# Attention values and probabilities held as rounded part and remainder side by side, multiplied head by head

## The reference

```python
def _L0_xattn_ref(x, context, ln_gamma, ln_beta, w_q, w_kv, w_out, b_out, gate):
    xn = _layernorm(x, ln_gamma, ln_beta)
    q = (xn @ w_q).reshape(B, SQ, NUM_HEADS, DIM_HEAD)
    k, v = jnp.split(context @ w_kv, 2, axis=-1)
    ...
    scores = jnp.einsum('bqhd,bkhd->bhqk', q * SCALE, k)
    attn = jax.nn.softmax(scores, axis=-1)
    out = jnp.einsum('bhqk,bkhd->bqhd', attn, v).reshape(B, SQ, INNER)
    return (out @ w_out + b_out) * jnp.tanh(gate[0])

x = x + jnp.tanh(g_xattn[0]) * _L0_xattn_ref(_layernorm(x, axis=-1), ctx_1024, ...)
```

## Time and profile before

| | us |
|---|---|
| median of three runs | 1162.66 |
| lowest and highest of them | 1161.47, 1164.37 |
| the profiled execution: device time | 1161.57 |
| the profiled execution: span of its trace | 1159.8 |
| busy in the span: PE / PEld | 1075.9 / 930.8 |
| busy in the span: DVE / ACT / POOL | 773.1 / 631.4 / 519.8 |

### The profile page before, as it was taken

The page is one execution under the profiler, slowest core; times in us unless marked ns, Lnnn a source line. Parts: engine busy times, 40 slices in busy tenths (PEclk is TensorE's granted clock), DMA queues, the critical chain, the costliest instruction groups (busy, mean ns, idle before and its releaser), DMA issues.

```text
span 1159.8 us, 22342 instructions
## 1 busy us (share of the span) xinstructions
PE 1075.9 (93%) x7361; PEld 930.8 (80%) x7361; DVE 773.1 (67%) x1963; ACT 631.4 (54%) x1676; POOL 519.8 (45%) x745
## 2 busy tenths in 40 slices
PE   3889999999999999999999999999999779899995
PEld 3688888888888888888788888888887668789983
DVE  2544677767676767776676777676766665686665
ACT  2533556555656565655556565656564545555650
POOL 3512345453535454454535354536354404565441
PEclk9989999999999999999999999999999888999998
DMA  5395882010101011010001010101000522234469
GB/s 150 96 329 207 309 297 63 5 34 9 30 27 31 27 31 35 23 35 22 23 16 32 8 38 9 31 9 31 5 18 9 176 83 78 99 108 152 133 198 287
DMA packets 82382, 95.82 MB, mean 83 GB/s; under 512 B 9291, under 2 KB 74445, under 8 KB 82272
## 3 DMA queue, kind: packets, MB, share of 16 engines
q1 hardware_dynamic: 41904, 44.94, 13.5%
q10 hardware_dynamic: 31520, 32.51, 7.9%
q0 software_dynamic: 8848, 16.96, 4.2%
HBM read 41.98 MB, written 52.39 MB: 81 GB/s over the span
## 4 chain that ended last, share of the span: by engine, by line
PE 61%; DVE 16%; ACT 10%; issue 6%; DMA 4%; POOL 3%; SPq 1%; DVEq 0%; ACTq 0%; POOLq 0%
PE ps_kv L1568 14%; PE ps_ot L1854 8%; PE ps_ot L1668 5%; PE ps_kv L1650 5%; PE ps_s L1811 5%; PE ps_pt L1821 5%; ACT prob L938 4%; DVE negmax L1467 3%; PE ps_pt L1780 3%; PE ps_ot L1793 3%; DVE pT_lo L1478 2%; DVE k_lo L1152 2%; ACT v_hi L928 2%; DMA zb<-places 2%; PE ps_ot L1712 2%
## 5 line engine op out<-in xcount | busy, mean ns | idle before, releaser
L855 POOL TENSOR_TENSOR prob<-prob,rinv 112x750 f32<-112x750 f32 x128 | 185.4, 1448 | 310.7 <-DVE rinv L1472 310.4
L938 ACT ACTIVATE prob<-ps_s,negmax 112x375 f32<-112x375 f32 x256 | 144.7, 570 | 236.4 <-DVE negmax L1467 236.4
L1478 DVE TENSOR_TENSOR pT_lo<-ps_pt,pT_hi 125x672 fp32r<-125x672 f32 x128 | 109.7, 857 | 77.0 <-ACT pT_hi L1051 77.0
L1568 PE MATMUL ps_kv<-ctxT_hi,wkv 128*128 128x376 f32 x512 | 141.6, 357 | 7.8 <-DVE v_lo L1156 3.8
L1467 DVE TENSOR_REDUCE negmax<-ps_s 112x2 f32<-112x750 f32 x128 | 119.0, 930 | 0.1
L1156 DVE TENSOR_TENSOR v_lo<-ps_kv,v_hi 125x512 fp32r<-125x512 f32 x96 | 66.4, 692 | 77.2 <-ACT v_hi L928 77.2
L1568 PE MATMUL ps_kv<-wkv,ctxT_hi 128*125 128x512 f32 x384 | 112.2, 414 | 3.6 <-DVE n_e L1116 2.3
L1821 PE MATMUL ps_pt<-ident,prob 112*125 112x112 f32 x768 | 104.9, 273 | 1.3 <-POOL prob L855 1.3
L814 POOL DMA_INDIRECT places<-ysb,place_i x72 | 70.3, 976 | 69.1 <-ACT ysb L1010 55.9
L1051 ACT ACTIVATE pT_hi<-ps_pt 125x672 fp32r<-125x672 f32 x128 | 93.5, 730 | 9.0 <-PE ps_pt L1821 1.0
L1821 PEld LDWEIGHTS ps_pt<-ident,prob 112*125 112x125 f32 x768 | 95.1, 191 | 1.7 <-POOL prob L855 1.7
(11 more groups left out here) (298 smaller groups left out, 2623.8 us busy)
## 6 DMA issues: line engine op xcount, KB each, us to landing
rows_by_expert<-stage_w ACTq DMA_DIRECT2D x16, 1920.0 KB, 7.3
xg<-rows_by_expert SPq DMA_DIRECT2D x72, 128.0 KB, 2.1
zb<-places SPq DMA_DIRECT2D x16, 448.0 KB, 15.0
arena<-in_L_ffn_mlp_w SPq DMA_DIRECT2D x24, 256.0 KB, 4.4
ctx_in<-in_ctx SPq DMA_DIRECT2D x16, 375.0 KB
acc<-in_L_xattn_w_kv SPq DMA_DIRECT2D x4, 512.0 KB, 13.1
stage_w<-in_L_ffn_mlp_w SPq DMA_DIRECT2D x8, 256.0 KB, 3.0
x_in<-in_x SPq DMA_DIRECT2D x16, 112.0 KB, 2.1
```

The source lines that it names most:

```text
L855: e_prob.done(eng.tensor_tensor(prob[0:TQ, p % 2, :, :], prob[0:TQ, p % 2, :, :], rinv[:, 2 * p:2 * p + 2].unsqueeze(2).broadcast_to([TQ, ...
L938: e_exp.done(eng.activation(prob[0:TQ, p % 2, half, :], S[0:TQ, half, 0:SK], ACT.Exp, bias=negmax[:, h:h + 1], accum_out=rowsum[:, h:h + 1]))
L1478: e_pt_lo.done(eng.tensor_tensor(pT_lo[:, :, :, :].rearrange("p h k t -> p h (k t)"), PT[0:KEYT, :, 0:NKEY * TQ], pT_hi[:, :, :, :].bitcas ...
L1568: last = eng.matmul(out_, lhs(i, k), rhs(j, k), start=(n == 1), stop=(n == KT * len(PASSES)))
```

## The change

The three passes are folded into the shape of the operands. `v_hi` and `v_lo` become one tile `vx`, in which the 64 columns of a head's rounded part stand beside the 64 of its remainder; `pT_hi` and `pT_lo` become one tile `pT`, with 112 columns of the rounded part beside 112 of the remainder, for each head and key tile. One matmul for a head and a key tile then gives a 128 x 224 result of four blocks: hi·hi, hi·lo, lo·hi, and lo·lo, which isn't used. A pair takes 2 x 3 = 6 matmuls of the same size, where there were 9.

The three blocks that count have to be added, and stand in different partitions and columns of PSUM. ACT copies the block lo·hi of both heads (partitions 64 to 127, 64 x 224 in all) into `o_part`, which lies in unused partitions of the tile `b2_all`, in place of its two copies of 64 x 112. DVE gets three new instructions for a pair: `o_part` = hi·lo + `o_part` (64 x 224), then, after a wait on its own semaphore `s_co`, `oT` = hi·hi + `o_part` for each head (64 x 112 each). They stand behind `pT_lo` of the following pair, in slot 2p + 5. `e_oT` is now signalled by DVE.

```diff
-        v_hi = t("v_hi", [128, NKEY, INNER], F32R)
-        v_lo = t("v_lo", [128, NKEY, INNER], F32R)
+        vx = t("vx", [128, NKEY, NH, 2, DH], F32R)
-        pT_hi = t("pT_hi", [KEYT, 2, NKEY, TQ], F32R)
-        pT_lo = t("pT_lo", [KEYT, 2, NKEY, TQ], F32R)
+        pT = t("pT", [KEYT, 2, NKEY, 2, TQ], F32R)
...
+        b2_all = t("b2_all", [128, D])
+        b2, o_part = b2_all[0:NE, :], b2_all[64:128, 0:2 * TQ].rearrange("p (h t) -> p h t", t=TQ)
+        O = OT[:, 0:4 * TQ].rearrange("p (h a t) -> p h a t", a=2, t=TQ)
...
# ScalarE
                         e_o.wait_ge(eng, st, p + 1)
-                        for half in range(2):
-                            rows_ = slice(64 * half, 64 * half + 64)
-                            last = eng.activation(oT[rows_, p, :], OT[rows_, half * TQ:(half + 1) * TQ],
-                                                  ACT.Copy)
-                        e_oT.done(last)
+                        e_part.done(eng.activation(o_part[:, :, :], O[64:128, :, 0, :], ACT.Copy))
...
# VectorE, behind pT_lo in the slot
+                for p in range(NP):
+                    st = due(g, AT_O[p] + 1)
+                    if st:
+                        e_part.wait_ge(eng, st, p + 1)
+                        co(eng.tensor_tensor(o_part[:, :, :], O[0:64, :, 1, :], o_part[:, :, :], ALU.add))
+                        co.wait_ge()
+                        for half in range(2):
+                            last = eng.tensor_tensor(oT[64 * half:64 * half + 64, p, :], O[0:64, half, 0, :],
+                                                     o_part[:, half, :], ALU.add)
+                        e_oT.done(last)
...
# TensorE
-                        for i, j in PASSES:
+                        for half in range(2):
                             for k in range(NKEY):
-                                last = eng.matmul(OT[:, 0:2 * TQ].rearrange("p (h t) -> p h t", t=TQ),
-                                                  vv[i][0:KEYT, k, p * 128:(p + 1) * 128],
-                                                  pT[j][:, :, k, :], start=(n == 1),
-                                                  stop=(n == NKEY * len(PASSES)))
+                                last = eng.matmul(OT[:, 2 * half * TQ:2 * (half + 1) * TQ],
+                                                  vx[0:KEYT, k, 2 * p + half, :, :].rearrange("p a d -> p (a d)"),
+                                                  pT[:, half, k, :, :].rearrange("p a t -> p (a t)"),
+                                                  start=(k == 0), stop=(k == NKEY - 1))
```

More of the change, by code:

```diff
@@ L337, in program @@
         gwT = t("gwT", [128, KT, NE])
-        b2 = t("b2", [NE, D])
+        b2_all = t("b2_all", [128, D])
+        b2, o_part = b2_all[0:NE, :], b2_all[64:128, 0:2 * TQ].rearrange("p (h t) -> p h t", t=TQ)
         cols = t("cols", [128, 5, KT])
@@ L423, in program @@
         s_ct = sem("s_ct")
+        s_co = sem("s_co")
         e_x = event("e_x", 1, 16)
@@ L441, in program @@
         e_oT = event("e_oT", NP)
+        e_part = event("e_part", NP)
         e_xb0 = event("e_xb0", 1)
@@ L467, in program @@
         qk = (qk_hi, qk_lo)
-        vv = (v_hi, v_lo)
-        pT = (pT_hi, pT_lo)
+        O = OT[:, 0:4 * TQ].rearrange("p (h a t) -> p h a t", a=2, t=TQ)
         AT_S = [2 * p for p in range(NP)]
@@ L927, in projection @@
                 if kind == "v":
-                    ins = eng.activation(v_hi[0:KEYT, n % NKEY, n // NKEY * 512:(n // NKEY + 1) * 512],
-                                         bank[0:KEYT, :], ACT.Copy)
+                    ins = eng.activation(vx[0:KEYT, n % NKEY, n // NKEY * NP:(n // NKEY + 1) * NP, 0, :],
+                                         bank[0:KEYT, :].rearrange("p (h d) -> p h d", d=DH), ACT.Copy)
                 ins.then_inc(kv_act, 1)
@@ L1051, in _ @@
                         e_pt_hi.done(eng.activation(
-                            pT_hi[:, :, :, :].rearrange("p h k t -> p h (k t)"),
-                            PT[0:KEYT, :, 0:NKEY * TQ], ACT.Copy))
+                            pT[:, :, :, 0, :], PT[0:KEYT, :, 0:NKEY * TQ].rearrange("p h (k t) -> p h k t", t=TQ),
+                            ACT.Copy))
                 for k in SLOT_TILES.get(g - LAST_BODY, ())[:1]:
@@ L1071, in _ @@
         def _(eng):
-            ch, ct = Chain(eng, s_ch), Chain(eng, s_ct)
+            ch, ct, co = Chain(eng, s_ch), Chain(eng, s_ct), Chain(eng, s_co)
             def setup(n):
@@ L1154, in projection @@
                 if kind == "v":
-                    at = slice(n // NKEY * 512, (n // NKEY + 1) * 512)
-                    ins = eng.tensor_tensor(v_lo[0:KEYT, n % NKEY, at], bank[0:KEYT, :],
-                                            v_hi[0:KEYT, n % NKEY, at].bitcast(F32), ALU.subtract)
+                    own = vx[0:KEYT, n % NKEY, n // NKEY * NP:(n // NKEY + 1) * NP, :, :]
+                    ins = eng.tensor_tensor(own[:, :, 1, :], bank[0:KEYT, :].rearrange("p (h d) -> p h d", d=DH),
+                                            own[:, :, 0, :].bitcast(F32), ALU.subtract)
                 ins.then_inc(kv_dve, 1)
@@ L1478, in _ @@
                         e_pt_lo.done(eng.tensor_tensor(
-                            pT_lo[:, :, :, :].rearrange("p h k t -> p h (k t)"),
-                            PT[0:KEYT, :, 0:NKEY * TQ],
-                            pT_hi[:, :, :, :].bitcast(F32).rearrange("p h k t -> p h (k t)"),
-                            ALU.subtract))
+                            pT[:, :, :, 1, :], PT[0:KEYT, :, 0:NKEY * TQ].rearrange("p h (k t) -> p h k t", t=TQ),
+                            pT[:, :, :, 0, :].bitcast(F32), ALU.subtract))
+                for p in range(NP):
[8 more added lines that the diff above has]
+                        e_oT.done(last)
                 for k in SLOT_TILES.get(g - LAST_BODY, ())[:1]:
@@ L1849, in _ @@
                         e_oT.wait_ge(eng, st, p)
-                        n = 0
-                        for i, j in PASSES:
+                        for half in range(2):
                             for k in range(NKEY):
-                                n += 1
-                                last = eng.matmul(OT[:, 0:2 * TQ].rearrange("p (h t) -> p h t", t=TQ),
-                                                  vv[i][0:KEYT, k, p * 128:(p + 1) * 128],
-                                                  pT[j][:, :, k, :], start=(n == 1),
-                                                  stop=(n == NKEY * len(PASSES)))
+                                last = eng.matmul(OT[:, 2 * half * TQ:2 * (half + 1) * TQ],
+                                                  vx[0:KEYT, k, 2 * p + half, :, :].rearrange("p a d -> p (a d)"),
+                                                  pT[:, half, k, :, :].rearrange("p a t -> p (a t)"),
+                                                  start=(k == 0), stop=(k == NKEY - 1))
                         e_o.done(last)
```

## The result

The kernel with six matmuls and three additions a pair takes 1256.51 us (median of 4 runs, 1252.64 to 1257.93) against 1162.64 for the kernel before on the same chip (1161.47 to 1164.37). The ratio is 1.080, 95% interval 1.077 to 1.083. The forecast was 1254.6.

The account below looks back on a forecast made before the run. DVE and ACT's chain of waits bounds each 54.7 us batch from 605.9 to 626.6, PE the rest. Eight merges, 8.9 us, less 2.7 absorbed give 6.2; 15 x 6.2 = 93 on 1161.57 makes 1254.6 us, range 1185 to 1270.

Parts of the forecast that it names:

- Each DVE duration: The three new DVE additions: 0.386 us for 224 columns, 0.267 for each of 112, at 1.06 ns a column.
- The merge pushes its successor by 1.11 us: DVE queue behind pT_lo: without overlap, the three additions start the next instruction 1.89 us behind pT_lo instead of 0.78.
- PE's gain: Three matmuls fewer save 0.34 us a pair, counting for five of eight O, where PE leads: 1.7 us a batch.
- The walk: Lateness followed through the eight pT_lo of a batch, DVE's delays passed on through ACT: 6.2 us more, 60.9 for 54.7.
- The output projection now waits ... 1.4 us late: PE's output projection at 654.69 waits for the last pair's merge until 656.1, 1.4 us late.
- 620.85: again: The pT_lo at 620.85, in the DVE stretch, takes another full merge less 0.04 of ACT: lateness +3.2 us.
- The ends: First batch's heads and last tail, outside the 15 repeated stretches: 2.7 us of gain and as much loss, so nothing.
- Rival (a): Additions on DVE overlap, so a merge costs 0.80 us: 15 x 3.8 = 57 us more, 1219; chance 0.27.
- Rival (b): PE's stretch keeps its slack and DVE's waits there hide the merges: +1.3 us a batch, 1181; chance 0.15.
- (c): Merges fall into DVE's idle time everywhere and PE's gain is kept: -1.7 us a batch, 1136, faster; chance 0.06.
- (d): No change: gain and loss meet, within 3.5 us of 1162, needing three merges at about 0.6 us; chance 0.04.
- Strided writes: Writes of vx and pT might cost more as well, making the kernel worse than 1270 us; chance 0.03.

Follow-up runs that it names:

- run 3: Changed kernel with o_part and the three additions' results all at partition 0, so no vector instruction changes partitions (result not the reference's): 1207.94 us, ratio 1.039.
- run 1: Changed kernel without the three DVE additions: six matmuls a pair, two ACT copies of hi x hi alone, remainder products left out: 1132.65 us, ratio 0.975.
- run 5: Changed kernel with seven small filler matmuls on PE before the last output projection of each batch, nothing left out: 1248.62 us, ratio 1.075.
- run 7: Kernel before, with GpSimd's product of prob and rinv covering only the first head of each pair, second head's scaling left out: 1150.9 us, ratio 0.990.
- run 6: Changed kernel with the three DVE additions ahead of pT_lo in their slot instead of behind it, same work and result: 1174.44 us, ratio 1.009.
- run 2: Kernel before, keeping nine matmuls, plus the changed kernel's ACT copy and three DVE additions at the same places (result not the reference's): 1254.85 us, ratio 1.078.
- run 10: Kernel before, unchanged, traced once more on a chip where it runs slower: 1197.53 us (one run; 1198.1 as the median of 17 beside).

## Why the prediction was right, step by step

- **Each DVE duration** was right: 0.386 and 0.267 us from two rows of another shape, 0.384 and 0.267 measured. The ACT copy: 352 ns, 0.36 assumed.
- **The merge pushes its successor by 1.11 us**: 1.89 us instead of 0.78, to the hundredth. The terms of 0.03 between the instructions were estimates; in after the three gaps up to the last addition are 0.03, 0.04 (the wait on `s_co`) and 0.01 us, and 0.03 follow to the successor. The overlaps of the other sum were estimates too; in run 3 the steps from one start to the next are 0.41 (with 0.03 for the wait on `s_co`), 0.19 and 0.18, together 0.78 where the estimate has 0.80. The choice between 1.11 and 0.80 rested on an ACT row; run 3 shows for DVE that it is the start partition that decides, by 0.19 against 0.28 us for the same step. On ACT the new copy begins at 641.50, behind the end of its predecessor at 641.48, as was assumed.
- **PE's gain**: 1.7 us a batch if nothing else changes; run 1 measured 1.6. The 0.112 us a matmul, taken from rows of before, holds in after: six come in 0.66 us (679.29 to 679.95), 0.11 each.
- **The walk**, 6.2 us a batch. For one long batch (642.83 to 704.50, pair 7 to pair 7) the steps were, forecast then measured: 1.06 and 1.05 from pair 7 to 0; 0.35 and 2.06 over the output projection to pair 1 (0.37 in a short batch); 1.1 and 1.0 from pair 1 to 2; 1.05 and 0.16 to pair 3; 0.75 and 0.74; 1.1 and 1.1; 1.1 and 1.1; -0.3 and -0.2.
- **Two steps of it were wrong and nearly cancelled.** (i) "The output projection now waits ... 1.4 us late" was right as a wait and left out what it does to PE: the clock falls and the projections take 1.7 us more, in 7 of 15 batches (shown by run 5). (ii) "620.85: again" took the earlier trace rows's 613.82 to 620.85 as a stretch that a merge only lengthens. It held 0.9 us in which two one-column instructions were held up beside GpSimd, and the merge moved them out of it (run 7 gives back half of it by another way; the rest is read from the rows of after, 0.22 and 0.16 us where before had 0.63 and 0.67). As measured, 15 x 5.3 = 80 and 7 x 1.7 = 12 make 92; the forecast had 93. That the two errors, -13 and +12 us, met is luck, and the total is closer than its parts deserve. The ends, put at nothing, came to -1 us.
- **Rival (a)**, 1219, fell by the 1.89; run 3 is that case and gave 1208, lower than 1219 by the 15 x 0.9 us of (ii), which (a) lacks as well. **Rival (b)**, 1181, fell since PE's stretch lost its lead; its time comes near that of the other order of DVE's queue, run 6 (1174), where most merges do fall in DVE's idle time. Its mechanism doesn't: PE has only 25% of run 6's chain and DVE 44%, and one of the two full merges left, that of the step to pair 6, lies in what was PE's stretch. **(c) and (d)** needed more than that. Worth noting against my own text: I called the waits before `pT_lo` no cover for the merge, since they stand ahead of it, and did not ask what a merge placed there would cost.
- **Strided writes** cost nothing that shows (run 1). In after the subtractions into `pT` and `vx` take 854 and 688 ns, before 857 and 692; ACT's copies take 730 and 597, before 730 and 598.

## What to carry to other kernels

Whether an engine has room is read at the place in its queue where the new work goes: the same additions, with the six matmuls, cost 94 us behind `pT_lo`, 148 with seven of the eight merges behind `negmax` and 11 ahead of `pT_lo`, on an engine that was idle for 16 of 55 us before they came. Before moving work within a queue, list both who waits for what it holds up and who waits for its own result. And before a saving on the fullest engine is multiplied by the number of times it occurs, see in the chain for how many of them this engine leads: here about five of eight (run 1), and two once the additions are in (after beside run 2).

## What the runs showed of the hardware

- DVE instructions that all start at partition 0 (run 3) overlap by 0.08 us where no wait stands between them, those that change between partitions 0 and 64 (after) don't; there the next starts 0.01 to 0.03 us behind the end. It is 0.19 against 0.28 us from the second addition to the third, and 0.77 against 0.89 from `pT_lo` to the first. Eight merges of it are 2.3 us a batch. Between the first addition and the second stands the wait on `s_co`, with 0.03 to 0.04 us from end to start in both.
- On ACT, before's second copy to `oT`, which starts at partition 64, begins 0.01 us behind the first in all 128 pairs, where the first overlaps the instruction before it by up to 0.13 us.
- Two one-column DVE instructions with SBUF inputs (L1170 and L1172 in before) take 0.21 and 0.16 us with GpSimd idle. Beside GpSimd's product or `xb` they lasted until that had ended: 0.63 and 0.67 us in before and 0.69 in run 7, with ends 0.01 to 0.02 us behind the GpSimd end. Beside a GpSimd instruction of one column (0.55 us from 613.15) L1172 kept its 0.16 at 613.29. `pT_lo` and the additions, with one input from PSUM, kept their lengths beside the product and `xb`: 0.84 to 0.86 us for `pT_lo` in before, 0.38 and 0.27 for the additions in after.
- After a wait of PE of 1.68 us, ended at 651.53, the granted clock was 0.57 from 652.0 to 654.5; with that wait filled (0.17 us left, run 5) it stayed at 1.00. It happened in seven of the fourteen batches of after that have this wait; there the projection took 2.85 to 3.67 us, in the others 1.98. What picks them wasn't settled. In run 3 the wait was 1.33 to 1.35 us (0.61 in the first of the fifteen batches), and the projection took 1.98 in all fifteen.
- F32R against float32 on PE, in before: the matmuls of O, with 224 columns, follow each other every 0.112 us. The four of an output projection, float32 with 256 columns, take 1.82 us from 654.69 to the next start at 656.51, 0.455 each. That is 0.50 against 1.78 ns a column.
- The same kernel was 3% slower on two chips than on others, in all its runs (1199 against 1163 us). Idle time of 2 us a batch with no releaser on the core (29.2 us in 14 waits, run 10) makes 1.4 us a batch of it, some 20 of the 36 us; the rest lies in the expert products. What either is stays open.
